# The expert layers' order of work: fixed numbers replaced by an order of token counts, in a two-layer decoder with top-2 experts

## The reference

```python
x = x + attn(layernorm(x)); x = x + xattn(layernorm(x), ctx); x = x + ffn(layernorm(x))
# ffn, layer 0 (layer 1: softmax gates of the top 2, gelu, hidden 1024, biases)
top_v, top_i = top_k(x @ Wg.T, 2)
gating = softmax(where(chosen, logits, -inf))
hidden_e = silu(x @ W1[e].T) * (x @ W2[e].T)          # hidden 682
out = sum_e gating_e * (hidden_e @ W3[e].T)
```

| layer | after batch | tokens of experts 0 to 7 |
|---|---|---|
| 0 | 3 | 229, 247, 290, 394, 214, 242, 195, 237 |
| 0 | 4 | 366, 279, 428, 462, 221, 347, 208, 249 |
| 0 | 7 | 649, 346, 547, 601, 350, 646, 380, 577 |
| 1 | 3 | 221, 197, 249, 404, 300, 180, 331, 166 |
| 1 | 4 | 394, 199, 350, 468, 303, 345, 333, 168 |
| 1 | 7 | 713, 290, 477, 648, 442, 530, 725, 271 |

## Time and profile before

### The profile page before, as it was taken

How to read it: one execution, slowest core, us unless ns; L and a number is a source line. 1 busy time by engine, 2 the same in 40 slices (tenths; PEclk the granted TensorE clock), 3 DMA queues, 4 the chain that set the end, 5 groups by cost and what they waited for, 6 DMA issues and landing times. The chain is left out here.

```text
span 1560.6 us, 34654 instructions
## 1 busy us (share of the span) xinstructions
PE 1455.8 (93%) x11868; PEld 1172.6 (75%) x11869; DVE 744.2 (48%) x2124; ACT 621.6 (40%) x1721; POOL 492.8 (32%) x762
## 2 busy tenths in 40 slices
PE   7999978998999999959999999998799989999996
PEld 5667656767999999936777777776466679999996
DVE  6666646896433333325444444443278952222221
ACT  2333336663122222215445444544266543334332
POOL 4445431444322222213233223323124442222222
PEclk9999998999999999979999999999799989999999
DMA  9910030112243333220000000000301122533331
GB/s 317 333 42 2 2 116 8 36 56 70 52 141 89 90 88 86 34 60 1 1 1 1 1 1 1 1 1 1 114 9 49 53 76 37 145 95 88 96 88 26
DMA packets 80239, 97.82 MB, mean 63 GB/s; under 512 B 10715, under 2 KB 73155, under 8 KB 80131
## 3 DMA queue, kind: packets, MB, share of 16 engines
q1 hardware_dynamic: 65075, 77.98, 15.7%
q0 software_dynamic: 13824, 17.19, 6.4%
q10 hardware_dynamic: 1232, 1.18, 0.2%
HBM read 57.91 MB, written 39.72 MB: 63 GB/s over the span
## 5 line engine op out<-in xcount | busy, mean ns | idle before, releaser
L1496 POOL TENSOR_TENSOR L1a_prob<-L1a_prob,L1a_rtot 128x1024 f32<-128x1024 f32 x64 | 121.1, 1893 | 284.5 <-DVE L1a_rtot L1376 284.5
L1905 PEld LDWEIGHTS L0x_ps<-L0f_rows_t,L0f_w_up 128*128 128x128 f32 x1584 | 183.4, 193 | 12.0 <-issue 10.7
L1905 PE MATMUL L0x_ps<-L0f_rows_t,L0f_w_up 128*128 128x128 f32 x1584 | 185.8, 277 | 6.9 <-issue 4.4
L1973 ACT ACTIVATE L1f_hid<-L1x_ps,L1f_b_up 128x128 f32<-128x128 f32 x304 | 95.0, 363 | 171.7 <-PE L1x_ps L1905 171.7
L1905 PEld LDWEIGHTS L1x_ps<-L1f_rows_t,L1f_w_up 128*128 128x128 f32 x1216 | 143.7, 194 | 4.5 <-issue 2.7
L1905 PE MATMUL L1x_ps<-L1f_rows_t,L1f_w_up 128*128 128x128 f32 x1216 | 145.0, 278 | 1.2 <-ACT L1f_rows_t L1957 1.2
L1914 PE MATMUL L1x_ps<-L1f_w_down,L1f_hid 128*128 128x256 f32 x608 | 137.8, 380 | 2.6 <-DVE L1f_y L2072 2.6
L1441 ACT ACTIVATE L1a_prob<-L1a_ps_s,L1a_nmax 128x256 f32<-128x256 f32 x256 | 118.2, 473 | 40.5 <-DVE L1a_nmax L1371 40.5
L1914 PEld LDWEIGHTS L1x_ps<-L1f_w_down,L1f_hid 128*128 128x128 f32 x608 | 112.7, 190 | 16.7 <-issue 3.0
L1116 POOL TENSOR_SCALAR_AFFINE_SELECT L0a_prob<-L0a_prob 128x128 f32<-128x128 f32 (+1 forms) x256 | 79.7, 353 | 104.5 <-ACT L0a_prob L1084 104.5
L1965 ACT ACTIVATE ctx_in<-L0x_ps 128x256 f32<-128x256 f32 x72 | 27.6, 383 | 187.1 <-PE L0x_ps L1905 187.1
(11 more groups left out here) (386 smaller groups left out, 2765.1 us busy)
## 6 DMA issues: line engine op xcount, KB each, us to landing
expert_table<-zero SPq DMA_DIRECT2D x1, 16640.0 KB, 68.5
L0f_w_up<-in_w_dram SPq DMA_DIRECT2D x8, 1408.0 KB, 6.3
L1f_w_up<-in_w_dram SPq DMA_DIRECT2D x8, 1024.0 KB, 5.0
L1f_w_down<-in_w_dram SPq DMA_DIRECT2D x8, 1024.0 KB, 7.6
L0f_w_down<-in_w_dram SPq DMA_DIRECT2D x8, 768.0 KB, 8.2
L1f_rows<-expert_table SPq DMA_DIRECT2D x36, 130.0 KB, 2.5
L0f_rows<-expert_table SPq DMA_DIRECT2D x34, 130.0 KB
sums<-X SPq DMA_DIRECT2D x8, 256.0 KB, 2.1
```

The lines of the kernel that those rows point to most:

```text
L1496: eng.tensor_tensor(v, v, r.unsqueeze(2).to_broadcast([P, 2 * QT_N, S]), ALU.mult).then_inc(norm_done, 1)
L1905: ins = eng.matmul(ps_h[c][:, o:o + P], w_up[par][:, t, w0:w0 + P], rows_t[:, t, :], start=(t == 0), stop=(t == DT - 1))
L1973: ins = eng.activation(hid[:, c, k * P:(k + 1) * P], ps_h[c][:, k * P:(k + 1) * P], ACT.Gelu, bias=b_up[par][:, 2 * c + k:2 * c + k + 1])
```

## The change

The experts are no longer taken by their numbers. After batch 3, DVE ranks them by tokens so far, most first, a tie to the lower number (`order`); place p in that order holds expert `expert[p]`. The early blocks are blocks 0 and 1 of places 0 and 1. Those of place 0 are loaded when batch 3 has been scattered, those of place 1 after batch 4 (`FULL_BY`), each with a semaphore of its own, and each held against its own snapshot. The main pass and its list go by places; SP reads the expert's number from memory before each load of weights. The weights of places 0 and 1 are loaded behind the order, no longer at the stage's start. Row numbers are compared with the tokens left of an expert (`left`) in place of absolute places. Temporaries of the list lie in the weights of the first self-attention, which are no longer used. `attention_quads` begins with 8 products of the identity on PE.

```diff
-def attention_crossed(nc, name, env, q_scale, wq, wk, wv, wo, bq, bk, bv, bo, w_landed, route, other_loads, experts):
+def idle_products(eng, out, ident, n):
+    for _ in range(n):
+        eng.matmul(out[:, 0:P], ident[:, :], ident[:, :], start=True, stop=True)
+def attention_crossed(nc, name, env, q_scale, wq, wk, wv, wo, bq, bk, bv, bo, w_landed, route, experts):
...
-                other_loads(eng)
                 for b in range(B):
...
-                    if b == SNAPSHOT + 1:
-                        for par in range(2):
-                            eng.wait_ge(scattered[par], ((SNAPSHOT - par) // 2 + 1) * 64)
-                        experts["load_early"](eng)
+                    if b == FULL_BY[0]:
+                        experts["first_loads"](eng)
+                    for i, last in enumerate(FULL_BY):
+                        if b == last + 1:
+                            for par in range(2):
+                                eng.wait_ge(scattered[par], ((last - par) // 2 + 1) * 64)
+                            experts["load_early"](eng, i)
...
                             slots(b - 3)
-                            if b - 3 == SNAPSHOT:
-                                experts["snapshot"](eng)
+                            for i, last in enumerate(FULL_BY):
+                                if b - 3 == last:
+                                    experts["snapshot"](eng, last)
...
-                    if b == SNAPSHOT + 1:
-                        eng.wait_ge(*experts["early_landed"])
+                    for i, last in enumerate(FULL_BY):
+                        if b == last + 1 and tiles[0] == 0:
+                            eng.wait_ge(*experts["early_landed"][i])
...
+                idle_products(eng, ps_o, ident, 8)
                 for e in FIRST:
                     make(0, e)
...
+    def in_order(eng, out, v):
+        linked(eng, eng.tensor_tensor(table8[:, :, :], which[:, :, :], outer(v), ALU.mult))
+        linked(eng, eng.tensor_reduce(out, table8[:, :, :], AX.X, ALU.add))
+    def count_tokens(eng):
+        linked(eng, eng.tensor_tensor(tokens[:, :], route["taken"][:, :], env["regions"][:, :], ALU.subtract))
+    def order(eng):
+        ids = route["experts"][:, :]
+        count_tokens(eng)
+        linked(eng, eng.tensor_scalar(by_place[:, :], tokens[:, :], float(EXPERTS), None, ALU.mult))
+        linked(eng, eng.tensor_tensor(by_place[:, :], by_place[:, :], ids, ALU.subtract))
+        linked(eng, eng.tensor_tensor(table8[:, :, :], outer(by_place[:, :]), inner(by_place[:, :]), ALU.is_gt))
+        linked(eng, eng.tensor_reduce(rank[:, :], table8[:, :, :], AX.X, ALU.add))
+        linked(eng, eng.tensor_tensor(which[:, :, :], inner(ids), outer(rank[:, :]), ALU.is_equal))
+        in_order(eng, expert[:, :], ids)
+        eng.tensor_copy(expert_i[:, :], expert[:, :]).then_inc(ordered, 1)
-    def snapshot(eng):
+    def snapshot(eng, last):
+        if last == FULL_BY[0]:
+            order(eng)
+        else:
+            count_tokens(eng)
+        in_order(eng, by_place[:, :], tokens[:, :])
         for k, (e, i) in enumerate(EARLY):
-            eng.tensor_scalar(full[:, k:k + 1], route["taken"][:, e:e + 1], float((e * REGION + i + 1) * P), None, ALU.is_ge)
+            if FULL_BY[e] == last:
+                eng.tensor_scalar(full[:, k:k + 1], by_place[:, e:e + 1], float((i + 1) * P), None, ALU.is_ge)
...
     def compute(eng):
...
-        linked(eng.tensor_tensor(tokens[:, :], route["taken"][:, :], env["regions"][:, :], ALU.subtract))
+        count_tokens(eng)
+        in_order(eng, by_place[:, :], tokens[:, :])
...
+        eng.tensor_scalar(start[:, :], expert[:, :], float(REGION), None, ALU.mult)
...
-        linked(eng.tensor_scalar(blocks_f[:, :], blocks_f[:, :], -1.0, float(REGION), ALU.mult, ALU.add))
-        linked(eng.tensor_tensor(blocks_f[:, :], blocks_f[:, :], done[:, 1:EXPERTS + 1], ALU.add))
-        linked(eng.tensor_tensor(blocks_f[:, :], blocks_f[:, :], done[:, 0:EXPERTS], ALU.subtract))
+        linked(eng, eng.tensor_tensor(start[:, :], start[:, :], done[:, :], ALU.add))
+        linked(eng, eng.tensor_tensor(blocks_f[:, 0:EXPERTS - 1], start[:, 1:EXPERTS], blocks_f[:, 0:EXPERTS - 1], ALU.subtract))
+        linked(eng, eng.tensor_tensor(blocks_f[:, 0:EXPERTS - 1], blocks_f[:, 0:EXPERTS - 1], start[:, 0:EXPERTS - 1], ALU.subtract))
...
-        eng.tensor_scalar(done[:, 0:EXPERTS], done[:, 0:EXPERTS], float(-P), None, ALU.mult).then_inc(link_v, 1)
+        linked(eng, eng.tensor_scalar(done[:, :], done[:, :], float(P), None, ALU.mult))
+        linked(eng, eng.tensor_tensor(by_place[:, :], by_place[:, :], done[:, :], ALU.subtract))
...
-        linked(eng.tensor_tensor(route["taken"][:, :], route["taken"][:, :], done[:, 0:EXPERTS], ALU.add))
...
-SNAPSHOT = 4
+FULL_BY = [3, 4]
...
+    def load_weights(eng, e, par):
+        weights["load"](eng, eng.value_load(expert_i[0:1, bass.ds(e, 1)], min_val=0, max_val=EXPERTS - 1), par)
+    def first_loads(eng):
+        eng.wait_ge(listed["ordered"], 1)
+        for e in range(2):
+            load_weights(eng, e, e)
-    def load_early(eng):
+    def load_early(eng, place):
+        number = eng.value_load(expert_i[0:1, bass.ds(place, 1)], min_val=0, max_val=EXPERTS - 1)
         for n, (e, i) in enumerate(EARLY):
-            first = (e * REGION + i) * P
-            eng.dma_start(early_rows[n][:, :], table[first:first + P, :]).then_inc(early_landed, 16)
+            if e == place:
+                eng.dma_start(early_rows[n][:, :], table[bass.ds(number * (REGION * P) + i * P, P), :]).then_inc(early_landed[e], 16)
...
-        experts_loop(eng, body, after=lambda e, par: weights["load"](eng, e + 2, par))
+        experts_loop(eng, body, after=lambda e, par: load_weights(eng, e + 2, par))
```

More of the change, by code:

```diff
@@ L1663, in block_list @@
+    which, table8 = (spare[:, 512 - EXPERTS * EXPERTS * k:512 - EXPERTS * EXPERTS * (k - 1)].rearrange("p (a b) -> p a b", a=EXPERTS) for k in (1, 2))
     list_f = tb("list_f", [P, LISTED])
[L1664 to L1668 removed]
+    done, full = tb("done", [P, EXPERTS]), tb("full", [P, len(EARLY)])
+    rank, expert, expert_i = tb("rank", [P, EXPERTS]), tb("expert", [P, EXPERTS]), tb("expert_i", [P, EXPERTS], I32)
@@ new lines, in block_list, with outer, inner, linked @@
+    link_v, made, ordered = (nc.alloc_semaphore(f"{name}_{n}") for n in ("link_v", "made", "ordered"))
+    n = [0]
+    def outer(v):
+        return v.unsqueeze(1).to_broadcast([P, EXPERTS, EXPERTS])
+    def inner(v):
+        return v.unsqueeze(2).to_broadcast([P, EXPERTS, EXPERTS])
+    def linked(eng, ins):
+        n[0] += 1
+        ins.then_inc(link_v, 1)
+        eng.wait_ge(link_v, n[0])
+    def in_order(eng, out, v):
+        linked(eng, eng.tensor_tensor(table8[:, :, :], which[:, :, :], outer(v), ALU.mult))
+        linked(eng, eng.tensor_reduce(out, table8[:, :, :], AX.X, ALU.add))
@@ L1712, in compute @@
         eng.tensor_tensor(list_i[:, :], list_f[:, :], env["numbers"][:, 0:LISTED], ALU.add).then_inc(made, 1)
-        eng.wait_ge(link_v, n[0])
-        linked(eng.tensor_tensor(route["taken"][:, :], route["taken"][:, :], done[:, 0:EXPERTS], ALU.add))
     route["list_blocks"] = compute
-    return dict(blocks=blocks_i, base=base_i, list=list_i, full=full, snapshot=snapshot, made=made, sems=[link_v, made])
+    return dict(blocks=blocks_i, base=base_i, list=list_i, expert=expert, expert_i=expert_i, left=by_place, full=full, snapshot=snapshot,
+                made=made, ordered=ordered, sems=[link_v, made, ordered])
@@ L1778, in moe @@
     early_rows = [spare[:, n * ROW:(n + 1) * ROW] for n in range(E)]
-    early_landed = sem("early_landed")
+    early_landed = [sem(f"early_landed{i}") for i in range(len(FULL_BY))]
+    of_expert = sum(e == 0 for e, _ in EARLY) * 16
     about = tb("about", [P, ROW - D])
@@ L2291, in load_tokens @@
                 eng.dma_start(X[:, tiles, :], summed[:, tiles, :]).then_inc(x_back[b], 16)
-        def first_experts(weights):
-            def loads(eng):
-                for e in range(2):
-                    weights["load"](eng, e, e)
-            return loads
         with ExitStack() as inner:
```

77 lines of the change are left out of this document (35 added, 42 removed).

## The result

Device time went from 1574.8 us (median of 6 runs, 1572.1 to 1579.6) to 1565.85 us (median of 6, 1563.6 to 1568.7): ratio 0.9941, 95% interval 0.9922 to 0.9960; 0.59% of 1574.8 is 9.3 us. A second set of runs gave 0.9952 (0.9933 to 0.9971). Forecast were 1565.2 and -9.4. The total was right and its parts were not: the reordered experts alone, without the fillers, gave 2.8 us in the mean where 8.4 were forecast (ratio 0.9995, 0.9973 to 1.0017, which is not told from no change), and the eight products of the identity some five times their forecast 1.0. That these two misses made up for each other is luck.

A forecast was written before the change was run, and what follows sets the result against it. PE was taken as the bound (busy 93%), its pace setting the expert main passes. Terms -7.25-2.0-3.2+0.6+1.5+2.0-1.0 = -9.4 us took the 1574.6 us median to 1565.2, range 1558 to 1573.

The forecast's parts named there:

- Blocks, -7.25: Second expert layer: fuller early experts need 37 blocks for 38, saving one block of PE time, 7.25 us.
- Reading the expert's number, +2.0: SP's register read before weight loads at six changes delays rows in the second layer: +2.0 us, bounds 0 and 3.5.
- Early rows, -4.5 and -5.7: Loop's end: place 0's earlier rows start up products sooner, clock kept; 4.5 us saved in the first layer, 5.7 second.
- the 1.4 and 3.8 us: Up products behind the loop: savings in first and second layer from TensorE keeping its clock through a shorter pause.
- The first weights, moved, +0.6: Weights loaded behind the order slow batch 3's last scatter 0.3 us per layer; rows and batch 4's send at about 357.
- Rival A: Batch 3's scatter lands only after all moved weights, stalling ScalarE 16 us in both layers: 1580.6 us; chance 0.10.
- Counting and ordering, +2.5 per layer: DVE's added work behind slots(3) and slots(4), less 0.85 us idle, ends the loop 2.5 us later per layer.
- The list, +1.5: Extra DVE list operations, 0.75 us in each layer, all on the path as PE waits: +1.5 us, bounds 0.8 and 3.
- Fillers, -1.0: Second self-attention's start: eight identity products raise PE's clock 3 us earlier for the first q and k: -1.0 us.
- Rival B: Only the block is won: clock falls in the shorter pause too and fillers give nothing: 1571.5 us; chance 0.17.

The follow-up runs named there:

- rows between: After, with the weights of place 1 issued behind the rows of place 0 in SP's queue, not ahead of them; ratio to before 0.9923.
- starts first: On rows between: DVE's memset and signals for the experts ahead of batch 5's slots, ACT's signal ahead of its table load; 1558.3 us, ratio to before 0.9885.
- rows late: After, with the rows of place 0 asked for together with those of place 1, after batch 4; ratio to before 0.9928.
- before again: The kernel before, unchanged, run and profiled a second time; ratio 1.0007, profiled execution 1576.5 us.
- after again: The kernel after, unchanged, run again beside the versions with other first transfers; ratio to before 0.9952.
- no fillers: After, without the eight products of the identity at the start of the second self-attention; ratio to before 0.9995, mean 1572.6 us.
- 4 fillers: After, with four products of the identity for eight at the start of the second self-attention; 1572.3 us, ratio to before 0.9972.
- block given back: After, with place 1's second early block in layer 1 counted as not full, so computed again (38 blocks for 37); ratio to before 1.0006.
- before with fillers: Before, with only the eight products of the identity added where the second self-attention begins; ratio to before 0.9981.

## Why the prediction was right in sum and wrong in its parts

*Blocks, -7.25.* Right: 37 for 38, 6.5 +-0.5 us (7.1 +-0.6 set by set).

*Reading the expert's number, +2.0.* The sum fits: 2.2 to 2.7 in layer 1's main pass; none in layer 0 (255.8 to 256.0 us in every trace). The reading of SP's register was not taken out by itself in any run, and the waits for rows hold only 0.8 to 1.7 of it.

*Early rows, -4.5 and -5.7.* This step failed, and it was the largest. "The turn can start at 360.4" and "the up products start at 362.4" took the rows for what held PE. The earlier trace rows has them as releaser of the turn, but the turn also needs ACT's signal behind the table load, 1.68 us behind the loop in rows between. The forecast 2.0 us had the turn run under that load and only the copy behind it; layer 1 takes 3.0. The up products behind it need the turned rows and DVE's `start`, which stands behind the last sums and the slots of batch 5 in DVE's queue and ran at 365.35 in the first trace of before too, behind the copied rows (364.87 + 0.38). DVE and ACT of that trace, in order of time:

```profile
365.16 0.17 DVE L356 CAST L0x_slot_i<-L0x_slot_f 128x4 int32<-128x4 f32 x1
365.35 0.17 DVE L2005 MEMSET L0f_hid<- 128x128 f32 x1
```
```profile
364.87 0.38 ACT L1957 ACTIVATE L0f_rows_t<-L0x_ps 128x256 f32<-128x256 f32 x1 [2.94 <-PE L0x_ps L1889]
```

The up products of the earlier trace rows began at 365.51: had the rows been there earlier, DVE would have let PE begin at the same time. With rows in place early the up products stayed at 4.95 us behind the loop in layer 0, and at 3.0 in layer 1 (2.8 to 4.1 in the traces with late ones). Nor was the clock kept, so the 1.4 and 3.8 us fell with it: in layer 0 the first 16 records took 3.75 us in starts first too, and in layer 1 only the first 8 ran at the upper level there (1.13 us), the next 24 took 4.77 for 4.11 in the earlier trace rows. What early rows are worth once both starts are moved is not shown, since rows late was not run on top of that.

*The first weights, moved, +0.6.* Forecast: "No cost", from rows and a send at about 357. The send came at 359.65: 4.35 MB of weights held all of the DMA engines until 358, and PE's last signals of the loop are late when the send's four scatters run over them (see below). That is 2.1 us in layer 0 and 0.3 to 2.1 in layer 1 (five traces), 2.5 by the two versions that avoid it. Rival A did not come: ScalarE's norm of batch 5 was released by POOL, 1.02 us, as in the earlier trace rows.

```profile
351.48 1.09 ACT L465 ACTIVATE L0x_xr<-X,L0x_r_shift_by,L0x_r_rstd 128x256 f32<-128x256 f32 x2 [1.02 <-POOL L0x_r_shift_by L597]
```

The last scatter of batch 3 was issued at 342.52 and held nothing at 351.48, while weights ran until 358. The rule that the prediction cited (the Trainium skill, "DMA: Bandwidth & Descriptors", Queues, rings and completion order: a DMA engine takes turns between its queues, packet by packet) fits that. It is about turns between queues; what cost here was rows on SP's own queue, behind the weights.

*Counting and ordering, +2.5 per layer.* The work was sized right (2.6 us) and its place wrong: "its only idle time to speak of is 0.85 us" held in one execution. Measured +1.3 +-0.6 for both layers (+0.7 +-0.7 set by set).

*The list, +1.5.* PE's waits for it went from 0.65 to 1.01 us in layer 0 and from 2.59 to 2.99 in layer 1. From the first up to the first turned rows of the main pass, before again took 46.8 and 44.9 us, after 46.2 and 45.5. No more than 1.

*Fillers, -1.0.* The mechanism was right, the size was off by about five: I priced the first q and k alone. These gave 3 us against 0.8 of delay. The rest is clock later in the same stage, most of all at its end. The last 20 us of the stage in before again and in after:

```profile
1105.00:1125.00 20.00, 16.05 (x61) 11.28 (x60) 1.38 (x2) 1.79 (x3) 0.00 (x0) 0.63 0.00 0
```
```profile
1095.00:1115.00 20.00, 15.32 (x84) 11.11 (x84) 1.56 (x3) 3.06 (x6) 1.89 (x1) 0.91 0.00 1
```

Why eight products change the clock 400 us later, the runs do not show.

Rival B ("Only the block is won", 1571.5) is the nearest to the change without its fillers (1572.2 measured), and the sign given for it came, a granted clock of 0.50 behind the loop's end (1263 to 1270 us in after). But the fillers, which by it give nothing, did give. The ledger at equal clock, set by set, is -7.1 (block) +2.2 (main pass) +2.5 (first transfers) +0.7 (ordering) and about +0.5 (list): -1.2 where -1.9 +-0.4 was measured. With the terms taken across the sets (-6.5, +2.7, +1.3) it is +0.5 for -1.8. Either way the gap is within what these single terms can tell together.

## What to carry to other kernels

A wait's last releaser in one row is not the chain: before a transfer is moved earlier, ask of the *next* instruction what else it waits for, and how long that has been done. Take the idle time in which new work is to hide from more than one execution, and set each time beside its granted clock; a microsecond of edit can shift the clock by more than it costs. Where PE waits behind a barrier, find the amount of filler work by trial: four products gave nothing, eight gave 5 us where 1 was forecast, and not in every execution alike.

## What the runs showed of the hardware

**PE's completions can come late while POOL issues indirect transfers.** PE in order of time, after, just ahead of DVE's row at 344.55 above, which takes these scores:

```profile
340.41 0.81 PE L744 MATMUL L0x_ps<-L0x_k_s,L0x_q_raw 32*128 32x154 f32 x16 [0.25 <-ACT L0x_prob L528]
```

The records end at 341.22, DVE begins 3.3 us later, and that is 1.07 us behind the end of the send's fourth scatter (342.52 + 0.96). The loop's last values, ended at 363.4, reach DVE at 365.60, 1.09 us behind the scatter of 363.55 + 0.96. The waiting row names "remote" or an unrelated DMA. In the five traces whose send stands at the loop's end (after, after again, no fillers, 4 fillers, block given back) this holds in both layers: 0.9 to 1.1 us behind the fourth scatter. The pause behind slots(3) stands in all thirteen traces after the first, in both layers, and ends 0.8 to 1.1 us behind the fourth scatter, but for one (0.1 us, before with fillers, layer 1). ACT's wait behind the list of layer 0 ends with a transfer of results that POOL issues (403.26 + 1.60 and 405.01). It is not at every send: at 1219.92 DVE took scores amid the scatters of another batch with 0.29 us of idle time. Moving the send away from the loop's end took the pause there away (three versions and the two built on one of them); the mechanism is open, and so is why the first trace of before had none of the three.

**The time of whole runs goes with their mean granted clock** on unchanged code (0.962 to 0.975, over 18 us of time), and a small edit elsewhere can come with a mean that is 0.004 higher: the ordering on DVE, which adds work, was 3 us faster with it.
